# Reciprocals of a softmax turned by the store to DRAM, 2048 single elements per group, in place of a transpose on TensorE and a copy on VectorE

## The chip, the cores and the metric

The kernel runs on one core of a Trainium2 chip. The metric is the device time of one execution in microseconds. The time before is the median of three runs. The profile is of one further execution, whose own time stands beside its span.

## The reference, cut to what matters

A gated cross-attention block and a gated feed-forward block follow each other, for 8 batches of 512 tokens with 512 features. Only the first matters here:

```python
Q, K, V = proj(layernorm(x), q_w, q_b), proj(ctx, k_w, k_b), proj(ctx, v_w, v_b)   # 16 heads of 32
scores = einsum('bhqd,bhkd->bhqk', Q, K) / sqrt(32)
scores = where(attn_mask, -1e9, scores)
attn = softmax(scores, axis=-1)
ctx = einsum('bhqk,bhkd->bhqd', attn, V)
x = x + tanh(g_xattn[0]) * (ctx @ o_w.T + o_b)
x = x + tanh(g_ffn[0]) * ffn(layernorm(x))
```

The kernel does not divide the probabilities by their sum. It multiplies unnormalised exponentials by V and scales the result by the reciprocal of each query's sum. That reciprocal is what is moved here.

## The kernel before, in words

**Tiles and groups.** A group is four heads of one batch: 16 tiles of 128 queries by 512 keys, four tiles for each head. A batch has four groups, c = 0 to 3, and there are 32 groups in a row (8 batches). After them comes the second stage (the projection of the attention's output and the feed-forward part), whose first steps are woven into the last batch.

**A tile.** TensorE makes the scores (L622) three tiles ahead. VectorE adds the mask and takes the row minimum of the negated scores (L1089). ScalarE takes the exponential and its sum (L914), two tiles ahead of the step. TensorE turns the tile so that the keys lie on the partitions (L631), and VectorE (even tiles, L1095) or ScalarE (odd tiles, L921) copies it out of PSUM. "Step" i of a group is what each engine does for tile i. Between these TensorE makes the projections of later groups, "side" items Q, K and V, whose order is a table written by hand (PE_SIDE, ORDER); each takes the next of two side banks in PSUM. After step 15 comes `context` (L643), 32 matmuls of the turned tiles with V, which waits until all copies of the group are done.

**The reciprocals.** At step 14 VectorE takes the reciprocals of the 16 sums of each of 128 query rows (L1101): `rden`, 128 partitions by 16 columns. The result of `context` has the features on the partitions and the queries along the row, so the reciprocals are needed the other way round and the same for the 32 features of a head. Before the change that is a side item of its own, "R": TensorE turns `rden` to 16 by 128 (L608), VectorE copies it to SBUF (L1060), SyncE's queue stores it to DRAM as 16 rows of 512 bytes (L440, `store_rden`), waits until that has landed, and loads it back four times, each head's 512 values to 32 partitions (L448, `spread_rden`, into `rden_bc`). At step 12 of the next group VectorE multiplies (`divide`, L1081), and the queue stores the result (L436).

Another small store, on ScalarE's queue and seven times in all, writes `mean_rstd` to `mr_dram` for the first layer norm (L886): 128 partitions, two runs each of four values, which is 256 pieces of 16 bytes.

**The queue.** All these transfers stand in one list on SyncE, in program order, and a wait in that list holds up all that is behind it. Between the store of the reciprocals and their loading back stand six loads of 256 KB, the Q and K of the next group (`load_bands`, L411). Behind the loading back stand stores of Q and K parts (L399, L401), the store of the previous result and, in the last batch, loads of the second stage's weights: with c = 2 `load_w2(3)` (L432, the matrix `wvvT`, into a buffer called w_raw in the trace) and `load_w2r` (L427). GpSimd splits these weights (L1439, L1442), in the order o, k, v, r, and after them computes the inverse root of the second layer norm (L1343 to L1350), for which VectorE waits with `xh` (L1248), and for that TensorE waits with the first transposes of the second stage (L730).

Of the kernel before, what the change touches and what calls it, by code (L numbers as in the profile page):

```python
# [25 lines left out]
P = 128  # L26
# [61 lines left out]
def stats_at(nb):  # L88
# [12 lines left out]
                      [i[:2] for step in range(END) for i in pe_side[c].get(step, []) if i[2] == 0] + [("R", c)]]  # L101
# [25 lines left out]
def build(nc, x, ctxT, mask, g_xattn, g_ffn, wq, bq, wk, bk, wv, bv, wo, bo, wr, wkk, wvv, mur, muk, ident_d, xT_d, out,  # L127
# [11 lines left out]
    with keep:  # L139
# [45 lines left out]
        rden_rows = [ctx_sb[0:TILES, s, 0:P] for s in range(2)]  # L185
# [97 lines left out]
        def side_no(b, item):  # L283

            return number(b, item, "CTKQVR")

        def side_bank_of(b, item):
            if (b, item) == (None, ("V", 0)):
                return first_v_bank
            if item in T_ITEMS:  # L290
                return turn_bank[item[1]]
            if (b, item) == (B - 1, ("R", GROUPS - 1)):
                return r_bank[0]
            return side_bank[side_no(b, item) % SIDE_BANKS]

        o_bank = [side_bank_of(B - 1, item) for item in (("V", GROUPS - 1), ("R", GROUPS - 2))]

        def mm_no(b, item):

            return number(b, item, "TKQVR")  # L300
# [36 lines left out]
        def _(sp):  # L337
# [100 lines left out]
            def store_rden(b, c):  # L438
                sp.wait_ge(side_done, done(side_no(b, ("R", c))))
                sp.dma_start(rden_dram[b * GROUPS + c].rearrange("(r q) -> r q", r=TILES),  # L440
                             rden_rows[c % 2]).then_inc(rden_st, 16)
# [9 lines left out]
            def batch(b):  # L451
                more = not is_last(b)
                for c in range(GROUPS):
# [8 lines left out]
                    if g:  # L462
                        store_rden(*previous)
# [11 lines left out]
                    if g:  # L475
                        spread_rden(g - 1)
# [76 lines left out]
        def _(pe):  # L553
# [15 lines left out]
            def side(b, kind, n, part, of):  # L569
# [34 lines left out]
                if kind == "R":  # L604
                    if is_last(b) and n == GROUPS - 2:
                        pe.wait_ge(x1_done, 1)
                    pe.wait_ge(rden_ready, b * GROUPS + n + 1 + HEAD)
                    mm = nc.tensor.transpose(bank[0:TILES, 0:P], rden[:], ident[:])  # L608
# [86 lines left out]
            def batch(b):  # L695
                for c in range(GROUPS):
                    for i in range(TILES):
                        if i and not (is_last(b) and c == GROUPS - 1 and i + AHEAD_S >= TILES):
                            scores(b, c, i + AHEAD_S)
                        for item in listed(PE_SIDES, b, c, i):  # L700
                            side(b, *item)
                        if is_last(b):
                            first_unit(c, i)
                        transpose_probs(b, c, i)
                    for item in listed(PE_SIDES, b, c, TILES):
                        side(b, *item)
                    if is_last(b):
                        first_unit(c, TILES)
                    if not (is_last(b) and c == GROUPS - 1):
                        scores(b, c, TILES + AHEAD_S)  # L710
                    side(b, "R", c, 0, 1)
                    context(b, c)
# [9 lines left out]
            def first_turned(m):  # L722

                if m == 0:
                    pe.wait_ge(x1_done, UM)
                if m == 1:
                    pe.wait_ge(side_done, done(side_no(B - 1, ("R", GROUPS - 2))))
                pe.wait_ge(xh_done, m + 1)
                for a in range(CH):
                    mm = nc.tensor.transpose(o_bank[m][:, a * P:(a + 1) * P], xh[:, m, a * P:(a + 1) * P], ident[:])  # L730
                mm.then_inc(t_mm, 1)

            def first_o_proj(h, m, part, of):

                bank = o_bank[1 - m if h == 0 else m]
                if part == 0:
                    pe.wait_ge(w2_lo_done[0], 1)
                    pe.wait_ge(c2_lo, h + 1)
                    if h == 1:
                        pe.wait_ge(xT_done, m + 1)  # L740
                    else:
                        pe.wait_ge(side_done, done(side_no(B - 1, (("R", GROUPS - 3), ("V", GROUPS - 1))[m])))
# [42 lines left out]
            def r_proj(b, h):  # L785
# [4 lines left out]
                if u == 0:  # L790
                    pe.wait_ge(side_done, done(side_no(B - 1, ("R", GROUPS - 1))))
# [32 lines left out]
        def _(act):  # L824
# [4 lines left out]
            def side(b, kind, n):  # L829
                item = (kind, n)  # L830
                bank = side_bank_of(b, item)
                if kind in "VR":
                    return
# [184 lines left out]
        def _(dve):  # L1018
# [28 lines left out]
            def side(b, kind, n):  # L1047
# [9 lines left out]
                if kind == "R":  # L1057
                    dve.wait_ge(side_mm, mm_no(b, item) + 1)
                    dve.wait_ge(ctx_st[n % 2], (b * 2 + n // 2) * 16 + DMA_HEAD)
                    nc.vector.tensor_copy(rden_rows[n % 2], bank[0:TILES, 0:P]).then_inc(side_done, 1)  # L1060
                    return
# [14 lines left out]
            def divide(b, c):  # L1076
# [3 lines left out]
                dve.wait_ge(pv_mm, g + 1)  # L1080
                nc.vector.tensor_tensor(ctx_sb[:, c % 2, :], pv_bank[:], rden_bc[:], ALU.mult).then_inc(ctx_done, 1)  # L1081
# [87 lines left out]
            def batch(b):  # L1169
                for c in range(GROUPS):  # L1170
# [15 lines left out]
                    if not (is_last(b) and c == GROUPS - 1):  # L1186
                        side(b, "R", c)
# [126 lines left out]
            side(B - 1, "R", GROUPS - 1)  # L1314
# [201 lines left out]
```

## Time and profile before

| | us |
|---|---|
| median of three runs | 1149.13 (1148.04 to 1149.97) |
| the profiled execution, its own time | 1148.36 |
| its span | 1146.6 |
| TensorE matmul busy | 1117.5 (97%) |
| VectorE busy | 868.7 (76%) |
| ScalarE busy | 684.6 (60%) |
| GpSimd busy | 366.3 (32%) |

The time of an execution is 1.8 us above its span. Busy times are sums over the whole span; the 32 groups of the attention take the first 783 us, and what a change in them is worth is read from a group's end, where the engines wait for each other. "Landing" of a DMA is the time from its issue on the queue until its last byte is reported.

### The profile page before, as it was taken

To read this page: it belongs to the slowest core of one execution; us is meant where nothing else is said; L and a number is where in the kernel's file an instruction comes from. 1 tells how busy PE (TensorE), PEld (TensorE's weight loads), DVE (VectorE), ACT (ScalarE), POOL (GpSimd) and SP (SyncE) were. 2 spreads that over 40 slices of the span, in tenths; PEclk is the share of its full clock that TensorE was granted. 3 is DMA by queue.
4 is the path that set the end of the run, shared out by engine and by line. 5 is a ranking of instruction groups with operands and counts; after the bars stand their busy time and mean duration, and the time that the engine had idled before them with its cause. 6 is when DMAs were issued, how large, how long until landed. Compare 5 with 4: busy or idle time off the path is not lost.

```text
span 1146.6 us, 21580 instructions
## 1 busy us (share of the span) xinstructions
PE 1117.5 (97%) x7216; PEld 897.7 (78%) x7216; DVE 868.7 (76%) x1964; ACT 684.6 (60%) x1527; POOL 366.3 (32%) x595
## 2 busy tenths in 40 slices
PE   5999999999999999999999999979999999999998
PEld 4778777778778778777877777857888888888887
DVE  6878887888788877887788778868666766666764
ACT  4767776777677777777778767755233322332232
POOL 0143144045036016215203501672443244323421
PEclk9999999999999999999999999989999999999999
DMA  8775675774775577457666457903221113111200
GB/s 271 201 199 148 179 212 140 194 198 134 193 202 151 161 201 208 131 168 217 160 186 194 139 151 204 263 21 102 72 94 56 56 56 109 57 55 55 75 19 37
DMA packets 95709, 162.48 MB, mean 142 GB/s; under 512 B 13296, under 2 KB 22640, under 8 KB 95472
## 3 DMA queue, kind: packets, MB, share of 16 engines
q1 hardware_dynamic: 84912, 143.37, 43.8%
q10 hardware_dynamic: 10688, 17.73, 5.4%
q8 instruction: 59, 0.97, 0.4%
q14 instruction: 50, 0.41, 0.1%
HBM read 109.91 MB, written 49.57 MB: 139 GB/s over the span
## 4 chain that ended last, share of the span: by engine, by line
PE 91%; DVE 2%; DMA 2%; POOL 1%; issue 1%; ACT 0%; SPq 0%; DVEq 0%; ACTq 0%; POOLq 0%
PE bank L562 30%; PE bank L631 18%; PE bank L593 14%; PE bank L622 10%; PE bank L643 9%; PE bank L601 8%; PE bank L756 1%; DMA w_raw<-wvvT 1%; DVE neg_s L1089 1%; DMA rden_dram<-ctx_sb 0%; POOL w2r_lo L1442 0%; POOL w2v_lo L1442 0%; PE bank L608 0%; PE bank L745 0%; DMA qk_dram<-k_lo 0%
## 5 line engine op out<-in xcount | busy, mean ns | idle before, releaser
L914 ACT ACTIVATE probs<-neg_s,negmax 128x512 f32<-128x512 f32 x512 | 367.9, 720 | 64.1 <-DVE negmax L1089 61.9
L1089 DVE CUSTOM_DVE_ANT_0 neg_s<-bank,mask_big 128x512 f32<-128x512 f32 x512 | 343.8, 679 | 9.6 <-DVE mask_big L1149 1.0
L631 PE MATMUL bank<-ident,probs 128*128 128x128 f32 x2048 | 308.0, 273 | 3.0 <-DVE pT L1095 3.0
L631 PEld LDWEIGHTS bank<-ident,probs 128*128 128x128 f32 x2048 | 248.4, 141 | 51.4 <-issue 6.3
L1095 DVE COPY pT<-bank 128x512 f32<-128x512 f32 x254 | 174.9, 688 | 110.3 <-PE bank L631 108.8
L622 PE MATMUL bank<-k_stack,q_stack 96*128 96x512 f32 x512 | 242.2, 474 | 0.0
L921 ACT COPY pT<-bank 128x512 f32<-128x512 f32 x258 | 149.7, 580 | 128.2 <-PE bank L631 127.4
L643 PE MATMUL bank<-pT,v_sb 128*32 128x512 f32 x1024 | 116.5, 595 | 0.6
L993 ACT ACTIVATE relu<-bank 128x512 f32<-128x512 f32 x32 | 19.1, 598 | 143.3 <-PE bank L562 141.3
L622 PEld LDWEIGHTS bank<-k_stack,q_stack 96*128 96x128 f32 x512 | 97.5, 190 | 1.1
L1429 POOL TENSOR_TENSOR o_sb<-o_sb,w_raw 128x1024 f32<-128x1024 f32 x15 | 36.6, 2442 | 189.6 <-DVE o_sb L1304 189.6
L914 ACT ACTIVATION_READ_ACCUMULATOR probs<-neg_s,negmax 128x1 f32 x512 | 96.9, 189 | 0.0
L1356 POOL COPY mean_rstd<-mv 128x4 f32<-128x4 f32 x7 | 1.3, 188 | 289.9 <-DVE mv L1045 289.9
L643 PEld LDWEIGHTS bank<-pT,v_sb 128*32 128x32 f32 x1024 | 31.3, 109 | 67.7 <-issue 67.7
L1362 POOL TENSOR_TENSOR x_rows<-x_rows 128x512 f32<-128x512 f32 x28 | 35.7, 1284 | 120.8 <-DMA x_rows<-mr_dram 79.0
L1220 DVE SCALAR_TENSOR_TENSOR w_raw<-bank,tg,x_in 128x512 f32<-128x512 f32 x32 | 23.4, 746 | 36.7 <-POOL o_sb L1429 36.6
L601 PEld LDWEIGHTS bank<-wv_lo,cT_hi 128*128 128x128 f32 x256 | 38.8, 190 | 15.3 <-issue 12.6
L593 PE MATMUL bank<-xT_lo,wq_hi 128*128 128x512 f32 x120 | 49.4, 412 | 0.0
L1286 DVE SCALAR_TENSOR_TENSOR kact<-bank,relu 128x512 f32<-128x512 f32 x32 | 22.1, 691 | 35.8 <-ACT relu L993 35.8
L593 PE MATMUL bank<-cT_lo,wk_hi 128*128 128x512 f32 x120 | 48.7, 406 | 0.0
L593 PE MATMUL bank<-cT_hi,wk_lo 128*128 128x512 f32 x120 | 47.4, 395 | 0.0
L593 PE MATMUL bank<-cT_hi,wk_hi 128*128 128x512 f32 x120 | 47.3, 394 | 0.0
(158 smaller groups left out, 2140.8 us busy)
## 6 DMA issues: line engine op xcount, KB each, us to landing
k_stack<-qk_dram SPq DMA_DIRECT2D x93, 256.0 KB, 5.3
q_stack<-qk_dram SPq DMA_DIRECT2D x93, 256.0 KB, 5.8
cT_raw<-ctxT SPq DMA_DIRECT2D x8, 1024.0 KB, 7.9
rden_bc<-rden_dram SPq DMA_DIRECT2D x128, 64.0 KB, 6.0
ctx_dram<-ctx_sb SPq DMA_DIRECT2D x32, 256.0 KB, 2.2
c_raw<-ctx_dram SPq DMA_DIRECT2D x16, 512.0 KB, 4.1
x_in<-x SPq DMA_DIRECT2D x16, 512.0 KB, 5.0
qk_dram<-k_hi SPq DMA_DIRECT2D x31, 256.0 KB, 2.7
```

The source lines that it names most:

```text
L562: mm = nc.tensor.matmul(dst, lhs(left, a), rhs(right, a), start=(part == 0 and a == 0), stop=(part == TERMS - 1 and a == CH - 1))
L593: mm = nc.tensor.matmul(bank[:], left[:, at // TERMS, cols], right[:, at // TERMS, :], start=(at == 0), stop=(at == TERMS * CH - 1))
L601: mm = nc.tensor.matmul(bank[:, k * UNIT:(k + 1) * UNIT], left[:, a, keys * P:(keys + 1) * P], right[:, a, n // 2 * UNIT:(n // 2 + 1) * UNIT],
L622: nc.tensor.matmul(s_bank[tile_no(b, c, i) % S_BANKS][:], stack[slot][0][:, j, q * P:(q + 1) * P], stack[slot][1][:, j, :], start=True, st ...
L631: mm = nc.tensor.transpose(pt_bank[i % 2][:, a * P:(a + 1) * P], probs[:, i % P_RING, a * P:(a + 1) * P], ident[:])
L643: mm = nc.tensor.matmul(pv_bank[j * HD:(j + 1) * HD, :], v_sb[:, a, head * HD:(head + 1) * HD], pT[:, j, a, :], start=(a == 0), stop=(a == ...
L914: nc.scalar.activation(probs[:, i % P_RING, :], neg_s[:, i % SM_RING, :], ACT.Exp, bias=negmax[:, k:k + 1], scale=-1.0, accum_out=den[:, g ...
L921: nc.scalar.copy(pT[:, j, :, q * P:(q + 1) * P], blocks(pt_bank[i % 2])).then_inc(pt_out[i % 2], 1)
L1089: nc.vector.tensor_tensor_reduce(neg_s[:, i % SM_RING, :], s_bank[tile_no(b, c, i) % S_BANKS][:], mask_big[:, q, :], 1.0, 3e38, ALU.add, A ...
L1095: nc.vector.tensor_copy(pT[:, j, :, q * P:(q + 1) * P], blocks(pt_bank[i % 2])).then_inc(pt_out[0], 1)
L1362: nc.gpsimd.tensor_tensor(x_rows[:, 2 + a % 2, :], x_rows[:, 2 + a % 2, :], x_rows[:, 0, :], ALU.subtract).then_inc(x_mid, 1)
L1429: nc.gpsimd.tensor_tensor(o_sb[:, h], o_sb[:, h], x1[h], ALU.add).then_inc(o_done, 1)
```

## The change

The side item R is gone from TensorE and VectorE, and with it its place in the order of the side banks. The store now reads `rden` itself, 128 partitions by 16 columns, and writes it turned: every value goes as a piece of 4 bytes to its own place in DRAM, 2048 pieces. In SyncE's list the store stands behind the six loads of the next group, directly ahead of the loading back, and waits for the reciprocals. Since `rden` is one buffer, VectorE's reciprocals wait until the store of the group before has landed, and `divide` takes over a wait on an older store.

```diff
-                      [i[:2] for step in range(END) for i in pe_side[c].get(step, []) if i[2] == 0] + [("R", c)]]
+                      [i[:2] for step in range(END) for i in pe_side[c].get(step, []) if i[2] == 0]]
...
             def store_rden(b, c):
-                sp.wait_ge(side_done, done(side_no(b, ("R", c))))
-                sp.dma_start(rden_dram[b * GROUPS + c].rearrange("(r q) -> r q", r=TILES),
-                             rden_rows[c % 2]).then_inc(rden_st, 16)
+                sp.wait_ge(rden_ready, b * GROUPS + c + 1 + HEAD)
+                sp.dma_start(rden_dram[b * GROUPS + c].rearrange("(r q) -> q r", r=TILES), rden[:],
+                             allow_slow_non_contiguous=True).then_inc(rden_st, 16)
...
-                    if g:
-                        store_rden(*previous)
                     if c == 0 and b == 0:
...
                     if g:
+                        store_rden(*previous)
                         spread_rden(g - 1)
...
-                if kind == "R":
-                    if is_last(b) and n == GROUPS - 2:
-                        pe.wait_ge(x1_done, 1)
-                    pe.wait_ge(rden_ready, b * GROUPS + n + 1 + HEAD)
-                    mm = nc.tensor.transpose(bank[0:TILES, 0:P], rden[:], ident[:])
...
-                    side(b, "R", c, 0, 1)
                     context(b, c)
...
-                if kind == "R":
-                    dve.wait_ge(side_mm, mm_no(b, item) + 1)
-                    dve.wait_ge(ctx_st[n % 2], (b * 2 + n // 2) * 16 + DMA_HEAD)
-                    nc.vector.tensor_copy(rden_rows[n % 2], bank[0:TILES, 0:P]).then_inc(side_done, 1)
-                    return
...
                 dve.wait_ge(pv_mm, g + 1)
+                dve.wait_ge(ctx_st[c % 2], (b * 2 + c // 2) * 16 + DMA_HEAD)
                 nc.vector.tensor_tensor(ctx_sb[:, c % 2, :], pv_bank[:], rden_bc[:], ALU.mult).then_inc(ctx_done, 1)
...
                 dve.wait_ge(p_exp, (g + 1) * TILES + SM_RING)
+                dve.wait_ge(rden_st, g * 16)
                 nc.vector.reciprocal(rden[:], den[:, c % 2, :]).then_inc(rden_ready, 1)
```

SyncE's list at the start of a group with c = 1, before (k_hi_st and the like are the landings of the stores of K and Q parts, s_mm counts tiles of scores, rden_st is the landing of the reciprocals' store):

```order
L401 DMA qk_dram<-q_lo 128x512 [waits side_done]
L440 DMA rden_dram<-ctx_sb 16x128 [waits side_done]
L411 DMA k_stack<-qk_dram 32x4x512 [waits k_hi_st,s_mm]
L411 DMA k_stack<-qk_dram 32x4x512
L411 DMA k_stack<-qk_dram 32x4x512 [waits k_lo_st]
L411 DMA q_stack<-qk_dram 32x4x512 [waits q_hi_st,s_mm]
L411 DMA q_stack<-qk_dram 32x4x512
L411 DMA q_stack<-qk_dram 32x4x512 [waits q_lo_st]
L448 DMA rden_bc<-rden_dram 32x512 [waits ctx_done,rden_st]
L448 DMA rden_bc<-rden_dram 32x512 x3
L399 DMA qk_dram<-q_hi 128x512 [waits side_hi]
```

The same place after the change:

```order
L398 DMA qk_dram<-q_lo 128x512 [waits side_done]
L408 DMA k_stack<-qk_dram 32x4x512 [waits k_hi_st,s_mm]
L408 DMA k_stack<-qk_dram 32x4x512
L408 DMA k_stack<-qk_dram 32x4x512 [waits k_lo_st]
L408 DMA q_stack<-qk_dram 32x4x512 [waits q_hi_st,s_mm]
L408 DMA q_stack<-qk_dram 32x4x512
L408 DMA q_stack<-qk_dram 32x4x512 [waits q_lo_st]
L437 DMA rden_dram<-rden 128x16x1 [waits rden_ready]
L445 DMA rden_bc<-rden_dram 32x512 [waits ctx_done,rden_st]
L445 DMA rden_bc<-rden_dram 32x512 x3
L396 DMA qk_dram<-q_hi 128x512 [waits side_hi]
```

The store has moved past six loads, and nothing stands any more between it and the loading back that waits for its landing.

SyncE's list in the last batch with c = 2, after the change, from the last load of Q; before it read the same but for the second row, which stood ahead of the six loads as there:

```order
L408 DMA q_stack<-qk_dram 32x4x512 [waits q_lo_st]
L437 DMA rden_dram<-rden 128x16x1 [waits rden_ready]
L445 DMA rden_bc<-rden_dram 32x512 [waits ctx_done,rden_st]
L445 DMA rden_bc<-rden_dram 32x512 x3
L429 DMA w_raw<-wvvT 128x4x512 [waits w2_lo_done1]
L424 DMA w2r_raw<-wrT 128x4x512 [waits side_mm]
```

The load of `wvvT` keeps its place behind the loading back, which now waits for the landing of a store that was issued just before it.

TensorE at the end of a group, before:

```order
L622 MATMUL bank<-k_stack,q_stack 128x512 [waits s_min]
L608 MATMUL bank<-ident,rden 16x128 [waits rden_ready,side_done]
L643 MATMUL bank<-pT,v_sb 32x512 [waits ctx_done,pt_out_odd,pt_out_even]
L643 MATMUL bank<-pT,v_sb 32x512 x15
L593 MATMUL bank<-xT_lo,wq_hi 128x512 [waits side_done]
```

In the changed kernel the second of these rows is gone, and `context` follows the scores directly.

## Rows read from the trace of the kernel before

**Rows 1.** The page: the chain that ended last, by engine.

```profile
PE 91%; DVE 2%; DMA 2%; POOL 1%; issue 1%; ACT 0%; SPq 0%; DVEq 0%; ACTq 0%; POOLq 0%
```

**Rows 2.** Waits of TensorE: us in total, times, longest.

```profile
PE bank L730 <- DVE xh L1248: 7.4, 1, 7.4
```

**Rows 3.** Timeline, end of a c = 1 group, ScalarE: start, duration, idle before.

```profile
447.24 0.72 ACT L914 ACTIVATE probs<-neg_s,negmax 128x512 f32<-128x512 f32 x1 [0.40 <-DVE negmax L1089]
...
447.96 0.56 ACT L921 COPY pT<-bank 128x512 f32<-128x512 f32 x1
```

**Rows 4.** Timeline, the same group's end, TensorE: the item R, then context.

```profile
448.46 0.27 PE L608 MATMUL bank<-ident,rden 128*16 128x128 f32 x1
448.67 1.06 PE L643 MATMUL bank<-pT,v_sb 128*32 128x512 f32 x8
```

**Rows 5.** Timeline, ends of a c = 3 and a c = 0 group, ScalarE's last copy.

```profile
401.90 0.56 ACT L921 COPY pT<-bank 128x512 f32<-128x512 f32 x1
...
424.81 0.56 ACT L921 COPY pT<-bank 128x512 f32<-128x512 f32 x1
```

**Rows 6.** Timeline, the same two ends, TensorE: context.

```profile
402.56 1.02 PE L643 MATMUL bank<-pT,v_sb 128*32 128x512 f32 x5
...
425.65 3.64 PE L643 MATMUL bank<-pT,v_sb 128*32 128x512 f32 x32
```

**Rows 7.** Timeline of SyncE: a c = 1 group, and the last c = 2.

```profile
433.05 1.76 SPq L448 DMA_DIRECT2D rden_bc<-rden_dram  x4
...
733.96 0.43 SPq L432 DMA_DIRECT2D w_raw<-wvvT  x1
```

**Rows 8.** Issues at 432.5, 710.9, 385.4, 499.4, 729.8 us: KB, landing.

```profile
q_stack<-qk_dram SPq DMA_DIRECT2D x1, 256.0 KB, 7.1
...
q_stack<-qk_dram SPq DMA_DIRECT2D x1, 256.0 KB, 7.0
...
k_stack<-qk_dram SPq DMA_DIRECT2D x1, 256.0 KB, 7.1
...
q_stack<-qk_dram SPq DMA_DIRECT2D x1, 256.0 KB, 6.6
...
q_stack<-qk_dram SPq DMA_DIRECT2D x1, 256.0 KB, 10.1
```

**Rows 9.** Timeline of VectorE: the divide that follows each of the first four.

```profile
444.65 0.68 DVE L1081 TENSOR_TENSOR ctx_sb<-bank,rden_bc 128x512 f32<-128x512 f32 x1
...
721.46 0.68 DVE L1081 TENSOR_TENSOR ctx_sb<-bank,rden_bc 128x512 f32<-128x512 f32 x1
...
398.59 0.68 DVE L1081 TENSOR_TENSOR ctx_sb<-bank,rden_bc 128x512 f32<-128x512 f32 x1
...
514.35 0.68 DVE L1081 TENSOR_TENSOR ctx_sb<-bank,rden_bc 128x512 f32<-128x512 f32 x1
```

**Rows 10.** Issues at 449.3, 752.9, 234.1 us, all seven of mr_dram, 699.9 us.

```profile
rden_dram<-ctx_sb SPq DMA_DIRECT2D x1, 8.0 KB, 1.3
...
rden_bc<-rden_dram SPq DMA_DIRECT2D x1, 64.0 KB, 2.0
...
mr_dram<-mean_rstd ACTq DMA_DIRECT2D x1, 4.0 KB, 1.6
...
mr_dram<-mean_rstd ACTq DMA_DIRECT2D x7, 4.0 KB, 2.3
...
w_raw<-woT SPq DMA_DIRECT2D x1, 1024.0 KB, 5.6
```

**Rows 11.** Busy time by stretch: engines, PEclk, DMA share, GB/s.

```profile
419.40:420.20 0.80, 0.80 (x7) 0.73 (x6) 0.80 (x4) 0.80 (x3) 0.00 (x0) 1.00 0.19 5
...
764.00:768.80 4.80, 4.80 (x20) 4.28 (x19) 3.79 (x9) 3.19 (x8) 4.59 (x4) 0.50 0.00 0
```

**Rows 12.** The chain that ended last, in order of time: start, us, what.

```profile
733.96 9.58 DMA w_raw<-wvvT
...
762.22 1.35 DVE xh L1248
```

More of the change, by code:

```diff
@@ L183, in build @@
         mean_rstd = sb(stage1, "mean_rstd", [P, 2, TT])
-        rden_rows = [ctx_sb[0:TILES, s, 0:P] for s in range(2)]
         mask_u8 = probs[:].rearrange("p r k -> p (r k)").bitcast(U8)[:, 0:TT * S].rearrange("p (t k) -> p t k", t=TT)
@@ L283, in side_no @@
         def side_no(b, item):
-            return number(b, item, "CTKQVR")
+            return number(b, item, "CTKQV")
         def side_bank_of(b, item):
@@ L291, in side_bank_of @@
                 return turn_bank[item[1]]
-            if (b, item) == (B - 1, ("R", GROUPS - 1)):
-                return r_bank[0]
             return side_bank[side_no(b, item) % SIDE_BANKS]
-        o_bank = [side_bank_of(B - 1, item) for item in (("V", GROUPS - 1), ("R", GROUPS - 2))]
+        o_bank = [side_bank_of(B - 1, item) for item in (("V", GROUPS - 1), ("V", GROUPS - 2))]
         def mm_no(b, item):
-            return number(b, item, "TKQVR")
+            return number(b, item, "TKQV")
         def hi_no(b, item):
@@ L725, in first_turned @@
                     pe.wait_ge(x1_done, UM)
-                if m == 1:
-                    pe.wait_ge(side_done, done(side_no(B - 1, ("R", GROUPS - 2))))
                 pe.wait_ge(xh_done, m + 1)
@@ L741, in first_o_proj @@
                     else:
-                        pe.wait_ge(side_done, done(side_no(B - 1, (("R", GROUPS - 3), ("V", GROUPS - 1))[m])))
+                        pe.wait_ge(side_done, done(side_no(B - 1, ("V", GROUPS - 2 + m))))
                 for at in share(TERMS * CH, part, of):
@@ L789, in r_proj @@
                 pe.wait_ge(recept_done, u * UM + HEAD)
-                if u == 0:
-                    pe.wait_ge(side_done, done(side_no(B - 1, ("R", GROUPS - 1))))
                 for m in range(UM):
@@ L831, in side @@
                 bank = side_bank_of(b, item)
-                if kind in "VR":
+                if kind == "V":
                     return
@@ L1185, in batch @@
                         side(b, kind, n)
-                    if not (is_last(b) and c == GROUPS - 1):
-                        side(b, "R", c)
                     if is_last(b):
@@ L1313, in _ @@
             mixed_lo(0, 0, 0)
-            side(B - 1, "R", GROUPS - 1)
             residual(0, 1, 1, o_bank[1])
```

## The prediction

> **What bounds the kernel now.** I read the page's chain first: 91% of it is TensorE [rows 1]. Then TensorE's waits: one long one in the whole program, 7.4 us at the start of the second stage, for `xh` of VectorE [rows 2]. The chain in order of time says what that wait hangs on: the load of `wvvT`, issued at 733.96, landed 9.58 us later at 743.5, then GpSimd's splitting, and VectorE's `xh` at 762.22 [rows 12]. So this load, far ahead of the wait, sets the end.
>
> Then the end of a group, where the waits are too short for a list. With c = 1 ScalarE's exponential stands 0.40 us for VectorE, and its copy of the last tile follows it and ends at 447.96 + 0.56 = 448.52 [rows 3]; TensorE does R at 448.46 and starts `context` at 448.67 [rows 4], 0.15 after that copy. With c = 3 the copy ends at 402.46 and `context` starts at 402.56, with c = 0 at 425.37 and 425.65 [rows 5, 6]: 0.10 and 0.28 after it. The 0.10 is the shortest, so I take it for the signal's travel: with c = 3 `context` waits for ScalarE, not for R. The reader should see that TensorE is "busy" throughout, yet at a group's end runs at the pace of the chain VectorE, ScalarE, copy.
>
> **What is removed.** R takes TensorE from 448.46 to 448.67, 0.21 us [rows 4], 32 times 6.7 us. Most of it is not to be had, since `context` cannot start earlier than 0.10 after the copy: 0.18 with c = 0, 0.05 with c = 1, nothing with c = 3, and nothing with c = 2, which I have not shown and take like c = 3. That makes 0.23 per batch, times 8, 1.8 us. VectorE's copy of R I cost at nothing: it stood behind the start of `context`, whose 32 matmuls give VectorE no tile to copy. If that cover failed, removing it would be a gain of at most as much as R's own. The side banks are taken in another order, but no row has TensorE waiting for one.
>
> **What is added: the store's own time, X.** The trace has no store of 4-byte pieces. The nearest is the store to mr_dram, 256 pieces of 16 bytes. The present store of the reciprocals, alone on the queue, lands in 1.3 us; mr_dram lands in 1.6 at best and 2.3 in the median [rows 10]. So 256 pieces cost 0.3 to 1.0 us, and eight times as many 2.4 to 8.0. From the other side: while those 256 pieces run, the DMA engines are busy 0.19 of 0.80 us, 0.15 us each [rows 11]; eight times that is 1.2 us, the lower end. I take X = 2.4, because a landing is waited for, not busy engines, and best against best leaves out other traffic. The SyncE queue holds the 2048 pieces behind the loads; ScalarE's queue is its own.
>
> By the page "DMA: Bandwidth & Descriptors" of the Trainium skill, section Rules for kernel authors, a plain DMA with a rearranged access pattern is 19 times slower than the hardware's transpose; taken on the store's whole landing it would make the sum 1751, against 1160 by the rows, and it is the last rival below. No run here shows a transpose by the DMA hardware, and the 256 pieces speak against so much.
>
> **Where it stands on the path.** The store is now issued after the six loads, and its pieces come behind theirs. The last load of a c = 1 group is issued at 432.5 and lands at 439.6 [rows 8]. Before, the four loads of `rden_bc` went out at 433.05 [rows 7], since their store had long been issued; now they wait until 439.6 + X. Four take 1.76 us to issue, so the last goes 1.3 later, and lands in 2.0 [rows 7, 10]: together X + 3.3 after the load's landing. `divide` starts at 444.65 [rows 9], a margin of 5.0. The others, in the same way [rows 8, 9]: the last c = 1 group lands at 717.9, divides at 721.46, margin 3.6; a c = 3 group 392.5 and 398.59, 6.1; a c = 0 group 506.0 and 514.35, 8.3; c = 2 I treat like c = 0. With X = 2.4 the need is 5.7: seven c = 1 groups are 0.7 late, the last 2.1, the rest not. What stands behind a late `divide` on VectorE: the mask and minimum of the next group's first tiles, the copy of tile 14, the reciprocals; ScalarE stands for those minima before its last copy, and `context` for that copy [rows 3, 4]. So a delay goes through in full: 7 x 0.7 + 2.1 = 7.0 us.
>
> **The load of wvvT.** With c = 2 of the last batch the last Q load lands at 729.8 + 10.1 = 739.9 [rows 8]. The four loads of `rden_bc` follow at 739.9 + X and take 1.8 us to issue, so `wvvT` goes out at 741.7 + X instead of 733.96 [rows 7]. By then the queue is empty, and a load of its size lands in 5.6 [rows 10], at 747.3 + X, against 743.5: 3.8 + X later, 6.2 us. The chain has nothing between this load and `xh` that could give it back [rows 12], so TensorE's 7.4 becomes about 13.6. In the stretch 764.0 to 768.8, after that wait, the granted clock is 0.50, the level of 1.2 GHz [rows 11], 4.8 us whose work would take 2.4 at the full one. A longer wait can use up that stretch (2.4 less) or lengthen it (as much more); I take neither.
>
> The other things behind the waiting store, the stores of K and Q parts, have their readers a group later and cost nothing; the loads back of the attention's output in the last batch move too and have GpSimd's splitting of other weights behind them, which is what could use up their slack.
>
> **The sum.** Against the profiled execution's 1148.4 (0.8 under the median of the runs): -1.8 + 7.0 + 6.2 gives 1159.8, so 1160.
>
> **The rivals.**
> *A quick store.* X is the busy time alone, 1.2. Then the seven groups are in time, the last is 0.9 late, and wvvT is 5.0 late: 1148.4 - 1.8 + 0.9 + 5.0 = 1152.5. With X near 0 it is 1150.4. For it: the busy share; against it: the landings.
> *A dear store.* X = 5: 7 x 3.3 + 4.7 + 7 x 2.2 = 43.2, wvvT 8.8, 1199; with X = 8.0, the median's price, c = 0 and c = 2 are 3.0 late too: 44.1 + 7.7 + 36.4 + 42.0 = 130.2, wvvT 11.8, 1289. For it: 256 pieces side by side may hide a slower end that 2048 show; against it: the 1.6.
> *Faster.* The margin holds everywhere and wvvT is not delayed, because the pieces are done beside the loads instead of behind them, so the store lands by 734 or so and the loading back goes out when it did. Then the gain of R alone is left, 1146.6, and down to 1148.4 - 6.7 = 1141.7 if `context` follows R's end and not the copy. It decides if the store issued behind six loads lands within about 1 us of them being issued; against it, the last load takes 7.1 to 10.1 to land from the same place.
> *Nineteen times.* The landing becomes 19 x 1.3 = 24.7, X = 23.4. Every group is late: 7 x 21.7 + 23.1 + 7 x 20.6 + 14 x 18.4 = 577, wvvT 27.2, 1751. That each piece is a transfer of its own would be the mechanism; 256 of them landing in 1.6 speak against it. This is the reading of the skill's rule named above.
>
> **How the numbers follow.** Forecast (X from 1.8 to 3.5) 0.42; quick store above 1151.4, 0.26; quick store with little else, inside 0.2%, 0.08; dear store 0.16; nineteen times 0.02; faster 0.06. The range goes from the quick store near 1151 to X = 5 at 1200 and leaves out the faster cases and the dearest. A difference under 0.2% (2.3 us) is about what a measurement cannot tell from none. So slower 0.86, same 0.08, faster 0.06.
>
> **What would show it.** In the profile after: `rden_bc` issued after the last load's landing plus 2.4; VectorE's `divide` waiting for a DMA in the c = 1 groups by 0.7, in the last by 2; no such wait with c = 0, 2; wvvT issued 10 us later and landing in 5.6; TensorE's wait for `xh` near 13.6; `context` 0.10 after the copy in every group. The prediction is wrong if the store's landing is not behind the loads, if X is past 4 (then c = 3 groups wait as well), or if VectorE has idle time between `divide` and the group's end that absorbs the delay.

## The result, and the profile after

The changed kernel takes 1329.1 us in the median of four runs (1327.2 to 1335.4), against 1149.0 for the kernel before on the same chip: 1.158 times as long, with an interval of 1.155 to 1.161. The prediction was 1160, in a range up to 1200: slower, as forecast, and far outside the range.

The profiled execution took 1327.2 us, its span is 1325.3. Its page, first the busy times, then the chain that ended last by engine and by line (the answer to [rows 1]), then a group of matmuls:

```profile
PE 1171.6 (88%) x7184; PEld 916.2 (69%) x7184; DVE 867.1 (65%) x1932; ACT 686.3 (52%) x1527; POOL 365.8 (28%) x595
...
DMA 40%; PE 39%; SPq 7%; DVE 5%; issue 4%; ACT 3%; POOL 1%; DVEq 0%; ACTq 0%; POOLq 0%
DMA rden_dram<-rden 27%; PE bank L558 25%; DMA rden_bc<-rden_dram 5%; PE bank L634 4%; SPq L408 3%; PE bank L622 3%; DMA qk_dram<-q_hi 3%; SPq L445 3%; DMA x_rows<-x 2%; PE bank L589 2%; DVE neg_s L1071 2%; PE bank L597 2%; PE bank L613 2%;
...
L634 PE MATMUL bank<-pT,v_sb 128*32 128x512 f32 x1024 | 151.0, 742 | 38.8 <-DVE pT L1077 37.4
```

TensorE, which was 91% of the chain, is 39% of it, and the turned store alone is 27%. The waits of SyncE, of VectorE and of TensorE (us in total, times, longest) say where it is felt; the last two rows answer to [rows 2]:

```profile
SPq L445 <- DMA rden_dram<-rden: 435.9, 32, 16.5
...
DVE ctx_sb L1063 <- DMA rden_bc<-rden_dram: 115.8, 26, 8.7
...
PE bank L613 <- DVE negmax L1071: 56.2, 19, 5.9
PE bank L634 <- DVE pT L1077: 37.4, 21, 2.1
PE bank L622 <- DVE pT L1077: 19.4, 12, 4.7
...
PE bank L718 <- DVE xh L1229: 9.9, 1, 9.9
PE bank L744 <- DVE xh L1229: 7.2, 1, 7.2
```

Of the waits for VectorE's tiles the trace of before has one, the counterpart of L622:

```profile
PE bank L631 <- DVE pT L1095: 3.0, 6, 0.9
```

SyncE now stands 13.6 us on average (435.9 / 32) for the landing of the store. `divide` stands for `rden_bc` in 26 groups of 32. TensorE's waits grow by 56.2 + 37.4 + 19.4 - 3.0 for VectorE and by 9.9 + 7.2 - 7.4 for `xh`, together 119.7. Its busy time grows by 1171.6 - 1117.5 = 54.1. The two make 173.8 of the 178.8 us by which the profiled execution is longer. 34.5 of the 54.1 is in `context`: 151.0 us of the last row above stood at 116.5 before. Its matmuls, duration in ns (least, median, most) and first and last start:

```profile
L634 PE MATMUL bank<-pT,v_sb x1024: 589/592/1063, 56.0 to 952.1; 128*32 128x512 f32 x171
```

The most was 617 before. The median is unchanged, the mean has gone from 595 to 742: some now run near twice as long. One group's end shows at which clock, first its `context` in TensorE's timeline, then a stretch of 2 us within it (us; busy time and count of TensorE, its weight loads, VectorE, ScalarE, GpSimd; granted clock; DMA share; GB/s):

```profile
427.04 6.54 PE L634 MATMUL bank<-pT,v_sb 128*32 128x512 f32 x32 [1.84 <-DVE pT L1077]
...
430.00:432.00 2.00, 2.00 (x12) 0.45 (x8) 0.00 (x0) 0.00 (x0) 0.00 (x0) 0.50 0.97 209
```

TensorE stood 1.84 us for VectorE, and then the 32 matmuls take 6.54 us, where they took 3.64 before [rows 6]; the granted clock within them is 0.50, the level of 1.2 GHz. The granted clock of the execution is 0.944, against 0.996 before.

SyncE's queue at the end of a group (start, us, what is issued), the answer to [rows 7]:

```profile
429.29 0.43 SPq L437 DMA_DIRECT2D rden_dram<-rden  x1
444.45 3.30 SPq L445 DMA_DIRECT2D rden_bc<-rden_dram  x4
```

From the store to the loading back it takes 15.2 us here, and 14.5 in the next group (the chain below). The same time by stretches (columns as above):

```profile
425.00:434.50 9.50, 7.66 (x42) 2.56 (x41) 3.15 (x10) 3.17 (x9) 4.54 (x5) 0.58 0.94 229
434.50:436.50 2.00, 2.00 (x17) 1.91 (x16) 1.68 (x4) 0.62 (x2) 0.00 (x0) 1.00 0.71 26
436.50:444.40 7.90, 7.90 (x57) 7.07 (x56) 7.23 (x19) 7.04 (x18) 4.26 (x6) 1.00 0.00 0
```

The loads keep the DMA engines busy until 434.5. The pieces follow, in 2 us. Then the DMA engines show nothing at all for 7.9 us, and only after that is the store's landing signalled. The cost is not the engines' busy time, which is what the lower bound was made of; it is a silence behind it. TensorE is not idle in that stretch, so no sum over engines shows it: the chain does. In order of time it goes round in a ring (start, us, what):

```profile
429.29 15.14 DMA rden_dram<-rden
...
447.33 1.99 DMA rden_bc<-rden_dram
449.34 0.04 DVE ctx_sb L1063
...
453.84 3.50 DMA qk_dram<-k_hi
459.23 14.51 DMA rden_dram<-rden
```

Store, loading back, `divide`, the minima and exponentials behind it, a K part, its store, the loads that need it, and behind those the next store. From one store to the next is 29.9 us; a group took 23 before. The first `divide` starts at 81.4 us and the last at 964.5 (before, 75.3 and 787.8), so 31 groups take 883.1 us in place of 712.5: 28.5 each instead of 23.0, and 170.6 of the 178.8 us.

At the end of the attention the chain answers to [rows 12]:

```profile
888.25 17.29 DMA rden_dram<-rden
...
907.30 6.00 DMA w_raw<-wvvT
...
931.87 1.35 DVE xh L1229
```

`wvvT` is issued 1.8 us after the loading back begins (905.55), lands in 6.0, and `xh` follows 18.6 later; before, it followed 18.7 after the landing.

### The profile page after: what moved, and what is told of

It is laid out like the page before. It is cut to its first block, busy times and chain, and to the rows that moved or that the text cites. A ratio compares the mean times of both kernels' runs of the same rounds, so it can differ in the third digit from the quotient of the medians.

```text
span 1325.3 us, 21450 instructions
## 1 busy us (share of the span) xinstructions
PE 1171.6 (88%) x7184; PEld 916.2 (69%) x7184; DVE 867.1 (65%) x1932; ACT 686.3 (52%) x1527; POOL 365.8 (28%) x595
## 4 chain that ended last, share of the span: by engine, by line
DMA 40%; PE 39%; SPq 7%; DVE 5%; issue 4%; ACT 3%; POOL 1%; DVEq 0%; ACTq 0%; POOLq 0%
DMA rden_dram<-rden 27%; PE bank L558 25%; DMA rden_bc<-rden_dram 5%; PE bank L634 4%; SPq L408 3%; PE bank L622 3%; DMA qk_dram<-q_hi 3%; SPq L445 3%; DMA x_rows<-x 2%; PE bank L589 2%; DVE neg_s L1071 2%; PE bank L597 2%; PE bank L613 2%; DMA qk_dram<-k_hi 1%; PE bank L744 1%
## 5 line engine op out<-in xcount | busy, mean ns | idle before, releaser
L622 PE MATMUL bank<-ident,probs 128*128 128x128 f32 x2048 | 312.8, 276 | 20.0 <-DVE pT L1077 19.4
L613 PE MATMUL bank<-k_stack,q_stack 96*128 96x512 f32 x512 | 249.7, 488 | 60.9 <-DVE negmax L1071 56.2
L622 PEld LDWEIGHTS bank<-ident,probs 128*128 128x128 f32 x2048 | 251.2, 142 | 71.2 <-issue 26.6
L634 PE MATMUL bank<-pT,v_sb 128*32 128x512 f32 x1024 | 151.0, 742 | 38.8 <-DVE pT L1077 37.4
L634 PEld LDWEIGHTS bank<-pT,v_sb 128*32 128x32 f32 x1024 | 42.0, 133 | 130.8 <-issue 83.8
L1063 DVE TENSOR_TENSOR ctx_sb<-bank,rden_bc 128x512 f32<-128x512 f32 x32 | 22.1, 690 | 115.8 <-DMA rden_bc<-rden_dram 115.8
L589 PE MATMUL bank<-xT_hi,wq_hi 128*128 128x512 f32 x120 | 48.8, 407 | 0.0
L589 PE MATMUL bank<-xT_hi,wq_lo 128*128 128x512 f32 x120 | 47.9, 399 | 0.0
```

Source lines behind the costliest of these rows:

```text
L589: mm = nc.tensor.matmul(bank[:], left[:, at // TERMS, cols], right[:, at // TERMS, :], start=(at == 0), stop=(at == TERMS * CH - 1))
L613: nc.tensor.matmul(s_bank[tile_no(b, c, i) % S_BANKS][:], stack[slot][0][:, j, q * P:(q + 1) * P], stack[slot][1][:, j, :], start=True, st ...
L622: mm = nc.tensor.transpose(pt_bank[i % 2][:, a * P:(a + 1) * P], probs[:, i % P_RING, a * P:(a + 1) * P], ident[:])
L634: mm = nc.tensor.matmul(pv_bank[j * HD:(j + 1) * HD, :], v_sb[:, a, head * HD:(head + 1) * HD], pT[:, j, a, :], start=(a == 0), stop=(a == ...
```

## The experiments

**The store by itself.** The kernel before, with 14 small DMAs behind its last output, each waited for before the next, so that the distance of two issues is a landing. The turned store is the fourth, L560.

```diff
...
+sp.dma_start(probe_dram[3, 0:2048].rearrange("(r q) -> q r", r=16), ident[:, 0:16], **slow).then_inc(probed, 16)
+sp.wait_ge(probed, 16 * 4)
...
```

> The kernel before, with fourteen small DMAs behind its last store, each waited for before the next, so that each is alone: 8 KB as 16 rows of 512 bytes, 128 rows of 64 bytes, 512 pieces of 16 bytes, 2048, 1024 and 512 pieces of 4 bytes written turned, 2048 pieces with 64 and with 512 bytes of DRAM to each, 2048 pieces in the order of the partitions 8 bytes apart, 1024 pieces of 64 and of 32 bytes, 2048 pieces into SBUF, 2048 pieces read from DRAM, and the 2048 turned again. Theory A (the number of short writes to DRAM sets the landing, about 5 ns each): 11 to 12 us for 2048 whatever the distance, 6 for 1024, 4 for 512, and 2 to 3 into SBUF and for full 64-byte pieces. Theory B (neighbouring pieces fall on the same lines of DRAM and wait for each other): 11 to 12 us for the turned 2048, but 2 to 4 with 64 or 512 bytes to each. Theory C (the descriptors are slow, wherever they go): 11 to 12 us for 2048 into SBUF and from DRAM as well.

SyncE's queue, from the third form on:

```profile
1150.59 0.37 SPq L558 DMA_DIRECT2D probe_dram<-ident  x1
1153.32 0.37 SPq L560 DMA_DIRECT2D probe_dram<-ident  x1
1164.23 0.36 SPq L562 DMA_DIRECT2D probe_dram<-ident  x1
1174.35 0.36 SPq L564 DMA_DIRECT2D probe_dram<-ident  x1
1183.80 0.36 SPq L566 DMA_DIRECT2D probe_dram<-ident  x1
1187.92 0.36 SPq L568 DMA_DIRECT2D probe_dram<-ident  x1
1191.77 0.63 SPq L570 DMA_DIRECT2D probe_dram<-ident  x1
1201.38 0.37 SPq L572 DMA_DIRECT2D probe_dram<-ident  x1
...
1205.95 0.67 SPq L576 DMA_DIRECT2D bv_row<-ident  x1
1208.89 0.37 SPq L578 DMA_DIRECT2D bv_row<-probe_dram  x1
```

The forms in their order: 16 rows of 512 bytes 1.4 us; 128 pieces of 64 bytes 1.4; 512 of 16 bytes 2.7; **2048 of 4 bytes, turned, 10.9**; 1024 turned 10.1; 512 turned 9.4; 2048 with a 64-byte place for each 4.1, with a 512-byte place 3.8. L570 is 2048 pieces in the order of the partitions, 8 bytes apart in DRAM: 9.6. L576 is 2048 pieces into SBUF, in that same order and 8 bytes apart: 2.9. 2048 read from DRAM take 2.8, and the turned store a second time 11.1. So neither the number of pieces nor their size as such is dear: 512 turned pieces take 9.4 where the same count of 16-byte ones takes 2.7, and the form that takes 9.6 into DRAM takes 2.9 into SBUF. What costs is short writes that lie close together in DRAM. The turned store shows the same silence as in the kernel, behind its first 2.6 us:

```profile
1155.90:1164.20 8.30, 0.00 (x0) 0.00 (x0) 0.00 (x0) 0.00 (x0) 0.00 (x0) 0.50 0.00 0
```

The Trainium skill, page "DMA: Bandwidth & Descriptors", section Specifications, says that below 512 bytes the DMA engine does a read-modify-write; section Why small descriptors are slow (HBM only) says that transfers from SBUF to SBUF don't suffer the penalty of small ones, which it puts down to fixed costs per packet and per descriptor. By this, the trace agrees in direction: 9.6 into DRAM against 2.9 into SBUF for the same form. But neither section tells the 10.9 from the 4.1, which are both 2048 writes of 4 bytes into DRAM.

**The place alone.** The kernel before, with its row store moved behind the six loads.

```diff
-                    if g:
-                        store_rden(*previous)
                     if c == 0 and b == 0:
...
                     if g:
+                        store_rden(*previous)
                         spread_rden(g - 1)
```

> The kernel before, with its 16 rows of 512 bytes stored behind the six loads instead of ahead of them; R stays on TensorE and VectorE. Theory of the pieces: the place costs only the delay of the wvvT load, 3.8 + 0.3 us by the sum of the prediction, and no divide is late: 1153. Rival, the place in the queue costs the time: near 1329.

1155.9 us (1154.7 to 1156.1), 1.0055 times as long as before (1.004 to 1.007). TensorE waits 12.1 us for `xh` in place of 7.4, and SyncE 192.9 us in 32 waits, 6.0 each, for the store. So the place costs some 6 us, most of it through `wvvT`; 1153 was expected. In one group the last load of Q is issued at 432.92 and the store at 433.27; their landings, and from the chain the load of `wvvT` (start, us, what):

```profile
DMA to landing us min/median/max: 6.8/6.8/6.8
...
DMA to landing us min/median/max: 6.7/6.7/6.7
...
745.74 5.42 DMA w_raw<-wvvT
```

So the row store lands right behind the last load, 0.2 us after it, and 0.2 is also the median of the 32 groups.

**A flat store at the new place.** The changed kernel, but every partition writes its 16 values in one piece. The reciprocals then stand in the wrong order, and the output is not the reference's.

```diff
-sp.dma_start(rden_dram[b * GROUPS + c].rearrange("(r q) -> q r", r=TILES), rden[:],
-             allow_slow_non_contiguous=True).then_inc(rden_st, 16)
+sp.dma_start(rden_dram[b * GROUPS + c].rearrange("(q r) -> q r", r=TILES), rden[:]).then_inc(rden_st, 16)
```

> The changed kernel, but the reciprocals are stored as they lie, 128 rows of 64 bytes, so that the output is not the reference's. Same bytes, same place, same waits, 128 pieces for 2048. Theory of the pieces: store to landing about 1 us more than 16 rows, no divide late, 1150 to 1153. Rival, the place or the waits: near 1329.

1155.5 us, 1.005 (1.0033 to 1.0066), some 2 us above what was expected; the wait for `xh` is 12.4. Same place, same bytes, no R: 174 us are gone with the pieces alone.

**The pieces at the old place**, ahead of the loads.

```diff
+                    if g:
+                        store_rden(*previous)
                     if c == 0 and b == 0:
...
                     if g:
-                        store_rden(*previous)
                         spread_rden(g - 1)
```

> The changed kernel, its 2048 pieces stored at the head of each group's list, ahead of the six loads. If the pieces cost only their own landing of about 11.5 us: rden_bc goes out at 438.5 instead of 433.05 in the c = 1 group, lands about 442, before the divide at 444.65; only wvvT is late, by about 6: 1153. If they also hold up the loads behind them, in the rings or in the memory, the loads land up to 9 us later, and the time lies between 1180 and 1329.

1284.4 us, 1.118 (1.115 to 1.1215). Were the store only late, ten microseconds more ahead of it should hide it. It does not, and the waits (us in total, times, longest) and landings name others that are late:

```profile
PE bank L614 <- DMA q_stack<-qk_dram: 27.8, 19, 7.0
...
SPq L405 <- DMA qk_dram<-q_hi: 96.2, 17, 9.6
...
q_stack<-qk_dram SPq DMA_DIRECT2D x93, 256.0 KB, 8.3
```

The loads of Q land in 8.3 us, against 5.8 before, and the stores of Q parts are waited for, 96.2 us in total, and those of K parts likewise, 68.0. So the pieces hold up transfers that have nothing to do with them, which my theory of a late `divide` did not contain. SyncE also stands 52.7 us here, in 30 waits, for the reciprocals, with the six loads behind it in the list; but the flat store at this place, below, has the same wait, stands 7.9 us in it and costs nothing, so it is the pieces that make it long.

**How near is near.** Again forms alone at the end, with 4 to 128 bytes of DRAM for each of 2048 turned pieces (`step` is 1 to 32 words of 4 bytes), and with 16 to 64 bytes in the order of the partitions, where a partition's own 16 pieces are neighbours.

```diff
+def turned(n, cols, step):
+    return probe_dram[n, 0:cols * P * step].rearrange("(r q t) -> q r t", r=cols, t=step)[:, :, 0]
...
+sp.dma_start(turned(1, 16, 2), ident[:, 0:16], **slow).then_inc(probed, 16)
...
```

> The kernel before, with fourteen DMAs of 4-byte pieces behind its last store, each alone: 2048 pieces written turned, with 4, 8, 16, 32, 64 and 128 bytes of DRAM to each; 2048 in the order of the partitions, with 16, 32 and 64 bytes to each; 128 pieces side by side; 128 pieces with 64 bytes to each; 16 pieces side by side; a single piece; and the turned 2048 again. Theory B, pieces that share a line of DRAM follow each other at about 0.5 us: 128 and even 16 side by side take 8 to 9 us, the single one and 128 apart 1.3 to 1.5, and the time falls by steps as the distance grows, halving where the pieces in a line halve (at 64-byte lines: 11, 6, 4, 4, 4, 4). Rival, something in the memory queue holds for a number of short writes whatever their lines: 16 pieces side by side land in under 2 us.

With 8 bytes for a piece 7.9 us, with 16 bytes 4.9, 32 bytes 4.9, 64 bytes 4.1, 128 bytes 4.4. 128 pieces side by side take 6.9, and 1.4 with 64 bytes each. So 128 side by side cost two thirds of 2048 (10.5 here). In the order of the partitions 2048 pieces take 9.5 with 16 bytes each, 6.7 with 32 and 5.2 with 64: the distance alone is not the measure, since at 16 bytes the turned order takes 4.9. Sixteen pieces side by side land in 1.3 and a single one in 1.0, which is the rival's sign; that neighbours follow each other at 0.5 us, as theory B had it, falls.

**The pieces apart, in the kernel.** The changed kernel with a 64-byte place for each piece; the loading back reads another tensor, so the output is not the reference's.

```diff
-sp.dma_start(rden_dram[b * GROUPS + c].rearrange("(r q) -> q r", r=TILES), rden[:],
+sp.dma_start(rden_dram[b * GROUPS + c].rearrange("(r q t) -> q r t", r=TILES, t=16)[:, :, 0], rden[:],
...
-                                 rden_dram[g:g + 1, j * S:(j + 1) * S].to_broadcast([HD, S])).then_inc(rden_ld, 16)
+                                 xT_d[g * GH + j:g * GH + j + 1, :].to_broadcast([HD, S])).then_inc(rden_ld, 16)
...
```

> The changed kernel, but each of the 2048 pieces goes to 64 bytes of DRAM of its own, and rden_bc is loaded from an input instead, with the same shapes and waits, so that the output is not the reference's. Alone this store lands in 4.1 instead of 10.9 us. Theory B: 2.8 us behind the last load, so the divide of the c = 1 groups is 1.1 late, of the last 2.5, wvvT 6.6: about 1166. Rival, the number of pieces among other traffic is what costs: near 1329.

1168.9 us, 1.019 (1.016 to 1.021). As many pieces, the same place, and 160 us less. The wait of SyncE for the landing:

```profile
SPq L445 <- DMA rden_dram<-rden: 253.9, 32, 11.3
```

That is 7.9 each, against 13.6 for the turned store and 6.0 for the row store at the same place. The prediction's X is the time from the landing of the last load to that of the store. Where the trace tells both, it can be read off, in the median of the 32 groups: 0.2 for the row store, 1.9 for the spaced pieces. For the changed kernel the trace doesn't tell the landings of the Q loads, and the waits give an estimate: 13.6 - 6.0 = 7.6 above the row store, so X is about 7.8. The 1166 expected here had been worked out with 2.8; that it was met so well with 1.9 is luck.

**Half the pieces**, those of two heads, loaded back twice; the output is not the reference's.

```diff
-sp.dma_start(rden_dram[b * GROUPS + c].rearrange("(r q) -> q r", r=TILES), rden[:],
+sp.dma_start(rden_dram[b * GROUPS + c].rearrange("(r q) -> q r", r=TILES)[:, 0:TILES // 2], rden[:, 0:TILES // 2],
...
-                                 rden_dram[g:g + 1, j * S:(j + 1) * S].to_broadcast([HD, S])).then_inc(rden_ld, 16)
+                                 rden_dram[g:g + 1, j % 2 * S:(j % 2 + 1) * S].to_broadcast([HD, S])).then_inc(rden_ld, 16)
```

> The changed kernel, but only the reciprocals of two of a group's four heads are stored, 1024 pieces, and loaded twice, so that the output is not the reference's. The pieces of a line of 64 bytes are as many as before. Theory B: the store lands at most 1 us sooner (10.1 against 10.9 alone), 28 groups give 0.5 to 1 each: 1300 to 1318. Theory A, the number of pieces: 5 us less to land, 28 times 4 to 5 less: 1190 to 1215.

1278.2 us, 1.113 (1.111 to 1.115). It lies between the two theories: halving the count takes 51 us of 180, less than a third, and 1278.2 lies outside what either had expected. A cost that grew with the count would have left some 90 of them. The store alone goes from 10.9 to 10.1.

**The chain behind `wvvT`.** The kernel before, with GpSimd's inverse root for `xh` ahead of a splitting of weights.

```diff
+            inverse_root2(0, 0)
             split_w2(2)
-            inverse_root2(0, 0)
```

> The kernel before, with GpSimd's inverse root of the first unit put ahead of the splitting of the weights r instead of behind it. If the load of wvvT and the splitting behind it set the end through xh, as the chain says, xh comes 7 us earlier, TensorE's wait of 7.4 and part of its stretch at half clock go: 1139 to 1143. If the weights r are wanted at once afterwards, nothing is won: 1149.

1148.8 us, 1.0001 (0.9991 to 1.001): nothing. One of TensorE's waits says why:

```profile
PE bank L745 <- POOL c_lo L1451: 7.2, 1, 7.2
```

The wait for `xh` is down to 0.5, and one of 7.2 for GpSimd's `c_lo`, some matmuls later, has taken its place. Both come from the list of work on GpSimd behind `wvvT`, and moving one item of it forward changes only which of them TensorE waits for.

**What makes them dear side by side.** Fourteen more forms by themselves. One theory was that a piece waits for another of the same DMA engine in the same short stretch of DRAM (a "line"); the other that all short writes into 512 bytes go one by one.

```diff
...
+sp.dma_start(probe_dram[2, 0:32].rearrange("(q r) -> q r", r=1), ident[0:32, 0:1], **slow).then_inc(probed, 16)
...
+sp.dma_start(probe_dram[4, 0:128].rearrange("(r q) -> q r", r=8), ident[0:16, 0:8], **slow).then_inc(probed, 16)
...
```

> The kernel before, with fourteen stores of 4-byte pieces behind its last one, each alone. 128, 64, 32 and 16 pieces side by side, one per partition; 128 pieces from 16 partitions so that neighbours in a line come from 16 different partitions; the same number from 16 partitions in order, 8 bytes apart; 2048 pieces from 16 partitions with 16 neighbours from different partitions; 128 pieces with 8, 16, 32 and 64 bytes to each; 256 side by side in two rows; the turned 2048; 128 again. Theory D (a write to DRAM that follows another write of the same DMA engine to the same line waits for it, about 0.9 us): 16 side by side 1.3, 32 about 2.2, 64 about 4, 128 about 7; 128 and 2048 pieces whose neighbours come from different partitions stay under 2 and near 4. Theory E (short writes into one stretch of 512 bytes go one by one, about 0.04 us each, whoever sends them): 1.3, 2.4, 3.8, 6.9, and 128 from 16 partitions 6.9 as well, 2048 from them 11.

```profile
1147.46 0.33 SPq L560 DMA_DIRECT2D probe_dram<-ident  x1
1154.79 0.49 SPq L562 DMA_DIRECT2D probe_dram<-ident  x1
1161.88 0.33 SPq L564 DMA_DIRECT2D probe_dram<-ident  x1
1165.22 0.32 SPq L566 DMA_DIRECT2D probe_dram<-ident  x1
1166.53 0.32 SPq L568 DMA_DIRECT2D probe_dram<-ident  x1
1172.87 0.62 SPq L570 DMA_DIRECT2D probe_dram<-ident  x1
```

One after the other: 128 side by side 7.3 us, 64 in 7.1, 32 in 3.3, 16 in 1.3, and 128 from 16 partitions, neighbours from different ones, 6.3. 2048 from 16 partitions in that way take 9.2. 128 pieces with 8, 16, 32 and 64 bytes each take 3.0, 2.1, 1.4 and 1.4; 256 in two runs 8.8; 2048 turned 11.8. Sixteen neighbours cost next to nothing, 16 to 64 cost 0.12 us a piece, and beyond that hardly anything. Neither theory holds. One by one into 512 bytes, 64 pieces should cost half of 128. By the other, the 128 from 16 partitions should have taken under 2 and 64 side by side about 4. What happens in the silence stays open.

**Pieces that nobody waits for.** The kernel before, its rows stored and loaded as ever, and behind the six loads of each group a turned store of 2048 values of `ident` to another tensor, waited for only a group later.

```diff
+                        sp.wait_ge(side_st, (g - 1) * 16)
+                        sp.dma_start(beside_dram[g - 1].rearrange("(r q) -> q r", r=TILES), ident[:, 0:TILES],
+                                     allow_slow_non_contiguous=True).then_inc(side_st, 16)
```

> The kernel before with its own turning and its own store in the old place, and in addition, behind the six loads of each group, the store of 2048 pieces (of a constant, to a tensor that nobody reads), for which nothing of the group waits. Theory of the waited landing: the pieces keep the DMA engines 1.2 us and no more, all margins hold: 1149 to 1153. Rival, the pieces also hold up the DMAs behind them while the memory works them off, 8 us in each group: 1170 to 1280.

1301.1 us (1296.1 to 1304.3), 1.131 (1.129 to 1.134). It costs nearly as much as the change, and more than the 1280 that the rival had allowed, though nothing in the kernel needs these pieces. VectorE's wait for `rden_bc`, SyncE's issues, and two stretches of the first of these groups (columns as above):

```profile
DVE ctx_sb L1085 <- DMA rden_bc<-rden_dram: 83.1, 27, 7.1
...
421.92 0.44 SPq L478 DMA_DIRECT2D beside_dram<-ident  x1
422.46 10.68 SPq L449 DMA_DIRECT2D rden_bc<-rden_dram  x4
...
450.50 8.61 SPq L449 DMA_DIRECT2D rden_bc<-rden_dram  x4
...
426.20:428.40 2.20, 2.20 (x20) 2.11 (x19) 1.88 (x6) 2.00 (x5) 0.15 (x1) 1.00 1.03 94
428.40:440.30 11.90, 11.90 (x75) 10.05 (x74) 8.80 (x23) 9.09 (x22) 7.14 (x8) 1.00 0.16 23
```

The pieces leave in 2.2 us. For the 11.9 us after them the DMA engines are busy 0.16 of the time and move 23 GB/s, though loads of `rden_bc` stand behind them; and issuing those four loads takes the queue 10.7 us and, in the next group, 8.6 (7.2 in the median of all groups), against 1.76 before [rows 7]. So what stands behind the pieces waits for them too.

The Trainium skill, page "DMA: Bandwidth & Descriptors", section Queues, rings and completion order, says that the increment of a semaphore is a strongly ordered write, which lands only after every earlier write of that DMA engine, across its queues. By that, a slow write delays the signals of all transfers behind it on the same engines; the late landings here and in the run with the pieces ahead of the loads agree with it. It does not by itself explain that so few packets run at all.

**The flat store at the old place**: without R, without the move, without the pieces; the output is not the reference's.

```diff
-                sp.dma_start(rden_dram[b * GROUPS + c].rearrange("(r q) -> q r", r=TILES), rden[:],
-                             allow_slow_non_contiguous=True).then_inc(rden_st, 16)
+                sp.dma_start(rden_dram[b * GROUPS + c].rearrange("(q r) -> q r", r=TILES), rden[:]).then_inc(rden_st, 16)
...
+                    if g:
+                        store_rden(*previous)
                     if c == 0 and b == 0:
...
                     if g:
-                        store_rden(*previous)
                         spread_rden(g - 1)
```

> The changed kernel with the reciprocals stored as they lie, 128 rows of 64 bytes, and at the old place ahead of the six loads, so that the output is not the reference's. It is the kernel before without R on TensorE and VectorE, and so the most that any other way to turn could win. Sum of the prediction: 1.8 us under before, 1146.5 to 1147.5. If context is bound by the copy everywhere: no difference. If R's time on TensorE came back in full: 6.7 less, 1142.

1147.8 us, 0.9988 (0.9979 to 0.9997). That is all that the removal of R brings, 1.4 us. Against the pieces at the same place (1284.4) it is 136.6 us less, with nothing else changed.

No version came out of this that computes the reference faster than the kernel before. A turn by a DMA from SBUF to SBUF, where 2048 pieces took 2.9 us, wasn't run.

## Why the prediction was wrong

**What R is worth: right.** 1.8 us were forecast for R, the flat store at the old place gained 1.4. VectorE's copy of R is in this figure, so it was worth nothing or nearly so, as costed. What bounds the kernel was read rightly but for one thing: `xh` alone does not set the end, since with `xh` early another item of GpSimd's list is waited for as long.

**The place of the store: right in kind, too small in size.** It was the store's landing, behind the loads, that the loading back waited for, in all 32 groups. With the row store's X of 0.2 the prediction's formula has no `divide` late and 3.8 + 0.2 = 4.0 for `wvvT`; the place alone measured 1155.9 - 1149.4 = 6.5. There the store ahead of `wvvT`, issued at 734.67, landed 9.12 later, at 743.8 in place of 740.1, and `wvvT` at 751.2, 7.6 later than before. In the changed kernel `wvvT` was issued 1.8 after the first load of `rden_bc` and landed in 6.0, where 5.6 was forecast. The faster rival fell: the pieces went behind the loads.

**The failing step: "I take X = 2.4".** It was scaled from the store to mr_dram, 256 pieces of 16 bytes and 0.3 us dearer than the row store, by the count of pieces. The turned store alone lands in 10.9 us, 9.5 above the row store, and in the kernel X is about 7.8. Put into the prediction's own formula this takes the forecast from 1159.8 to 1282.6, which is 122.8 of the 167.4 us that were missing. The count was the wrong measure. 512 pieces of 16 bytes land in 2.7, but 128 pieces of 4 bytes side by side in 7.3 already. What the two rows of before had no word on is how near the pieces lie to each other in DRAM, and in which order they are written. The upper bound of 8.0, from the median of mr_dram, came near the 7.8 by accident, and I gave it its place only as the far end of a rival at 0.16. The bound below, the busy share of the DMA engines, is refuted in kind: they are silent for most of the landing.

**The formula falls short as well.** With X = 7.8 a group needs 11.1: c = 1 is late by 6.1 seven times and 7.5 once, c = 3 by 5.0 seven times, c = 0 and 2 by 2.8 fourteen times, 124.4 in all; `wvvT` 11.6; R -1.8. That makes 1148.4 + 134.2 = 1282.6, against 1327.2, so 44.6 are missing. With the spaced pieces and X = 1.9 it gives 7 x 0.2 + 1.6 + 5.7 - 1.8 = 6.9, or 1155.3, and 1168.8 was measured. Where it goes wrong, three things can be named, but not priced one by one:
- It takes each delay against a schedule that otherwise stands. The chain shows a ring instead, in which the late `divide` makes the next K part late, and with it the next store.
- It left the clock out of the attention. TensorE's busy time grows by 54 us, and the granted clock of the execution is 0.944 against 0.996. That is a term of its own, which the prediction had named only for the stretch at `xh`.
- It let `wvvT` add to the rest. TensorE's wait for `xh` rose by 2.5 and one of 7.2 came behind it, 9.7 together, since the groups before had been late as well. This one goes the other way: the formula has 11.6 for it.

**What it did not have: the neighbours.** "The other things behind the waiting store ... cost nothing" was argued from their readers being a group away. The pieces hold up whatever runs behind or beside them: 1.131 with pieces that nobody awaits, 1.118 with the pieces ahead of the loads. How much of the 180 us is this and how much the late `divide` is not separated, since in the changed kernel both reach the same `divide`.

**The nineteen times rival** was too dear: 10.9 / 1.4 is 7.8 times the row store. The remark under it, that 256 pieces speak against so much, was the error of the whole sum: those pieces were of 16 bytes, and 4-byte ones side by side are another matter.

## What to carry to other kernels

Price a DMA by how close its short writes lie in DRAM and in which order, not by their number or by the engines' busy time: 4-byte writes side by side landed in 6 to 12 us from 64 of them on, with 64 bytes each in 1.4 to 5.2, and 2048 into SBUF in 2.9. If a trace has no transfer of that form, measure it alone before putting it into a loop, or widen the range to the far row. And look at what else is in flight behind it, because its landing was not the only one that it delayed.

## What the runs showed of the hardware that I had not expected

- The DMA engines show no packet for 8.3 us of the 10.9 in which a turned store of 2048 values lands.
- 16 pieces side by side cost hardly more than one (1.3 and 1.0 us), 64 cost as much as 128 (7.1 and 7.3), and 2048 only half as much again (10.5 to 11.8).
- At 16 bytes for each of 2048 pieces the order decides: 4.9 us turned, 9.5 with the pieces of a partition as neighbours.
- Behind such a store even the issue of the next loads stalls: four take 8.6 and 10.7 us instead of 1.76.
- In the changed kernel the small store to mr_dram on ScalarE's queue lands in 4.6 us in the median instead of 2.3 [rows 10], in a queue of its own. The row of the trace after:

```profile
mr_dram<-mean_rstd ACTq DMA_DIRECT2D x7, 4.0 KB, 4.6
```
